# Reordering hand-written engine tables of a four-layer sequence kernel: the turned x, the first MLP product, and the gate and up products of one pass

## The reference

```
# layer 0
mx = layernorm(x) * (1 + sc_msa) + s_msa
i, f, g = bitlinear(mx, wi), sigmoid(bitlinear(mx, wf)), bitlinear(mx, wg)
o = hgrn_scan(silu(i) * (1 - f), f)
o = rmsnorm(o) * silu(g)                      # u: the scan's output times the gate
x = x + g_msa * bitlinear(o, wo)
gate, up = split(bitlinear(mlp_in(x), wm1))
x = x + g_mlp * bitlinear(silu(gate) * up, wm2)
# layer 1
h = rmsnorm(x)                                # xn, turned to xT
z = h @ pre_w ;  g = smooth(z) * harmonic_gate
y = merge_w @ [h, style mixed by a cosine of g and style]
x = x + gelu(rmsnorm(y) @ ffn_w1) @ ffn_w2    # f1, gelu, f2
```

## Time and profile before

| | |
|---|---|
| median of 3 runs | 1957.49 us (1952.1 to 1957.84) |
| the profiled execution, device time | 1953.37 us |
| its span, first to last instruction | 1951.6 us |
| PE, DVE, ACT, POOL busy | 88%, 67%, 57%, 31% of the span |
| mean granted TensorE clock | 0.939 of full speed |

### The profile page before, as it was taken

How to read it: one execution, slowest core, us unless ns; L and a number is a source line. 1 busy time by engine, 2 the same in 40 slices (tenths; PEclk the granted TensorE clock), 3 DMA queues, 4 the chain that set the end, 5 groups by cost and what they waited for, 6 DMA issues and landing times.

```text
span 1951.6 us, 25700 instructions
## 1 busy us (share of the span) xinstructions
PE 1715.5 (88%) x8463; PEld 1015.6 (52%) x8463; DVE 1312.7 (67%) x2873; ACT 1112.6 (57%) x2118; POOL 611.0 (31%) x880
## 2 busy tenths in 40 slices
PE   2365576999989999988999999999999998999998
PEld 1144344667557657552445454544445444676766
DVE  5756877887876665577868686767686734656550
ACT  6644667878768763344675757565757564222221
POOL 0145655856645633610101010100001002334332
PEclk9755788989999999998999999999999999999999
DMA  9450000000000002303120303030303005000000
GB/s 375 123 167 1 24 6 20 20 1 20 15 1 14 20 4 67 66 18 68 26 47 11 61 2 71 2 68 5 68 5 68 5 3 152 3 11 22 12 22 22
DMA packets 94422, 83.57 MB, mean 43 GB/s; under 512 B 9881, under 2 KB 87842, under 8 KB 94034
## 3 DMA queue, kind: packets, MB, share of 16 engines
q1 hardware_dynamic: 94192, 81.91, 15.3%
q10 hardware_dynamic: 98, 0.03, 0.0%
HBM read 51.26 MB, written 5.09 MB: 29 GB/s over the span
## 4 chain that ended last, share of the span: by engine, by line
PE 41%; DVE 8%; ACT 6%; issue 1%; POOL 1%; POOLq 0%; DVEq 0%; ACTq 0%
PE k_psum L91 13%; PE k_psum L2536 6%; PE k_psum L2062 5%; PE k_psum L2123 5%; PE k_psum L2176 5%; PE k_psum L2053 4%; PE k_psum L97 3%; DVE l_small L2212 2%; ACT l_prob L2001 2%; ACT L2001 1%; ACT L2017 1%; ACT l_gu L2017 1%; DVE l_xn L2285 1%; DVE l_small L2199 1%; DVE l_xn L2287 1%
## 5 line engine op out<-in xcount | busy, mean ns | idle before, releaser
L2212 DVE TENSOR_REDUCE l_small<-k_psum 128x1 f32<-128x512 f32 x512 | 328.8, 684 | 124.6 <-PE k_psum L2176 121.7
L2001 ACT ACTIVATE l_prob<-k_psum 128x512 f32<-128x512 f32 x512 | 286.4, 596 | 196.6 <-PE k_psum L2053 193.4
L1985 POOL TENSOR_TENSOR k_x_res<-k_x_res,k_arena_a 128x256 f32<-128x256 f32 x32 | 23.3, 727 | 418.8 <-DVE k_arena_a L2256 418.8
L2062 PE MATMUL k_psum<-l_prob,l_v 128*32 128x512 f32 x1024 | 138.1, 612 | 0.2
L2123 PE MATMUL k_psum<-k_arena_a,l_gu 128*128 128x256 f32 x512 | 135.5, 393 | 0.7 <-ACT l_gu L2017 0.7
L91 PE MATMUL k_psum<-l_turned_over,k_arena_a 128*128 128x512 f32 x256 | 120.8, 596 | 4.2 <-ACT l_gu L2017 4.2
L91 PE MATMUL k_psum<-k_arena_b,l_w_f 128*128 128x512 f32 x256 | 123.9, 612 | 0.0
L1468 PE MATMUL k_psum<-l_w_f,k_arena_b 128*128 128x256 f32 x512 | 122.7, 386 | 0.2 <-ACT k_arena_b L1282 0.2
L91 PE MATMUL k_psum<-l_hT,k_arena_b 128*128 128x512 f32 x256 | 114.3, 592 | 0.0
L2536 PE MATMUL k_psum<-k_arena_b,l_gu 128*128 128x256 f32 x512 | 113.0, 379 | 0.0
L2123 PEld LDWEIGHTS k_psum<-k_arena_a,l_gu 128*128 128x128 f32 x512 | 97.9, 197 | 19.8 <-issue 2.2
(11 more groups left out here) (390 smaller groups left out, 3786.6 us busy)
## 6 DMA issues: line engine op xcount, KB each, us to landing
su_raw<-in_L_cond_wa SPq DMA_DIRECT2D x6, 1536.0 KB, 22.4
k_arena_b<-k_arena_c SPq DMA_DIRECT2D x32, 192.0 KB, 3.5
k_x_res<-in_x SPq DMA_DIRECT2D x1, 4096.0 KB, 19.7
k_arena_b<-k_arena_c SPq DMA_DIRECT2D x32, 128.0 KB, 3.2
out<-k_x_res SPq DMA_DIRECT2D x8, 512.0 KB, 2.9
l_mod_mlp<-mod SPq DMA_DIRECT2D x8, 384.0 KB, 3.6
l_qT<-k_arena_c SPq DMA_DIRECT2D x16, 192.0 KB, 3.7
l_kT<-k_arena_c SPq DMA_DIRECT2D x16, 192.0 KB, 3.2
```

Source lines behind the costliest of these rows:

```text
L2001: act.activation(prob[:, s % 2, j, :], psum[:, 2 + n % 2, :], ACT.Exp, scale=float(HD) ** -0.5).then_inc(exp_ready.sem, 1)
L2062: last = pe.matmul(psum[j * BLOCK:(j + 1) * BLOCK, 4, :], v[e % 2][:, kt, at:at + BLOCK], prob[:, n % 2, j, :], start=(kt == 0), stop=(kt ...
L2212: dve.tensor_reduce(mx[:, n % T, n // T:n // T + 1], psum[:, s_bank(e, n), :], AX.X, ALU.max).then_inc(max_ready.sem, 1)
```

## The change

Only the order of entries in three tables changes; no instruction is added or taken away, and every entry keeps its waits.

On ScalarE `xT` 0 moves from before `proj` 2 to behind it. On PE `turn` 0 moves behind `proj` 2 and one `f2` entry, and `turn` 1 behind `xq` 3 and one `f2` entry. In the middle of PE's pass `f1` 0 moves ahead of `up` 4, and `up` 5, 6 and 7 move behind `merge` 1, `f1` 1 and `merge` 2. On VectorE `h` 2 moves ahead of `s`, `rinv` and `base` 0; `u` 0, `h` 3, `u` 1, `merge` 0, `h` 4, `u` 2 are dealt anew, and `amax` 3 moves behind `u` 2.

```
 ACT_TURN
-    ... ("ssq2", 0, 0), ("ssq", 2, 2), ("xT", 0, -1),
-    ("proj", 2, 1), ("xl2", 3, 0), ("xT", 1, -1), ...
+    ... ("ssq2", 0, 0), ("ssq", 2, 2),
+    ("proj", 2, 1), ("xT", 0, -1), ("xl2", 3, 0), ("xT", 1, -1), ...
 PE_TURN
     ... ("gate", 5, 0),
-    ("mods", 1, 1), ("up", 4, 0), ("f1", 0, -2), ("up", 5, 0), ("gate", 6, 0), ("merge", 1, -1), ("gate", 7, 0), ("up", 6, 0), ("f1", 1, -2),
-    ("up", 7, 0), ("merge", 2, -1), ("f1", 2, -2), ...
+    ("mods", 1, 1), ("f1", 0, -2), ("up", 4, 0), ("gate", 6, 0), ("merge", 1, -1), ("up", 5, 0), ("gate", 7, 0), ("f1", 1, -2), ("up", 6, 0),
+    ("merge", 2, -1), ("up", 7, 0), ("f1", 2, -2), ...
-    ("f2", 2, -2), ("xq", 2, 2), ("f2", 3, -2), ("turn", 0, 0), ("proj", 2, 2), ("f2", 4, -2), ("turn", 1, 0), ("xq", 3, 2), ("f2", 5, -2),
+    ("f2", 2, -2), ("xq", 2, 2), ("f2", 3, -2), ("proj", 2, 2), ("f2", 4, -2), ("turn", 0, 0), ("xq", 3, 2), ("f2", 5, -2), ("turn", 1, 0),
     ("proj", 3, 2), ("pre", 0, 0))
 DVE_TURN
-    ... ("h", 1, -2), ("xw", 3, 0), ("s", 0, -3), ("rinv", 0, -3),
-    ("base", 0, -3), ("h", 2, -2), ("u", 0, -1), ("amax", 3, 0), ("u", 1, -1), ("h", 3, -2), ("merge", 0, -3), ("u", 2, -1), ("h", 4, -2),
+    ... ("h", 1, -2), ("xw", 3, 0), ("h", 2, -2), ("s", 0, -3), ("rinv", 0, -3),
+    ("u", 0, -1), ("base", 0, -3), ("h", 3, -2), ("u", 1, -1), ("merge", 0, -3), ("h", 4, -2), ("u", 2, -1), ("amax", 3, 0),
     ("amaxh", 0, -2), ("u", 3, -1), ("h", 5, -2), ...
```

## The result

The changed kernel takes 1984.87 us (median of 4 runs, 1980.06 to 1988.55) against 1957.66 us before (4 runs beside them): 1.0142 times as long, 95% interval 1.0109 to 1.0175, 27.2 us by the medians. The forecast was 1972, slower, with a range from 1957 to 1990: the result lies inside it, 12.9 us above the forecast. The profiled execution took 1988.55 us, its span is 1986.8 us. It is the slowest of the four, and its trace is 35.2 us longer than that of the kernel before, 8 us more than the medians differ: what follows is read from this one pair of executions. The page's first part, as in the earlier trace rows, hides it: TensorE is busy 20 us longer in a span that is 35 us longer.

The account below looks back on a forecast made before the run. The bound was a pass as one ring through PE, VectorE, ScalarE and GpSimd. 3 x 4.4 + 1.0 + 2.2 + 2.2 - 0.6 - 1.5 = +16.5 us on 1953.4, plus 2, gave 1972; range 1957 to 1990.

Parts of the forecast that it names:

- The ring: Whole pass: dots, MLP middle, `hq`, ScalarE and GpSimd, next pass; lengthening any part lengthens every pass.
- The middle of a full pass: Passes 2, 3, 6: late `h` 4, `u` 2, `silu` 5 make `gate` 6 wait 2.5 us; 4.4 us lost per pass.
- Passes 4 and 5 and the held `s`: `s` held by GpSimd's `hw` 0; 2.71 us wait at `up` 3 goes, `o` 3 waits 1.5; -0.3 us each.
- The end: End of pass: `turn` 0's wait nearly goes, but `fi` 0 waits for `proj` 3; 0.25 us gained in 6 passes, -1.5.
- Passes 0, 1, 6 and 7: Passes 0, 1 and 7 lack parts: 1.0, 2.2 and 2.2 us longer; pass 6 like 2 and 3, 4.4 us.
- clock rival: Clock falls after the new wait at `gate` 6: 3.5 us in passes 2 to 6, 17 us more, 1989; chance 0.20.
- the held `s` could not decide: Rival, faster: passes 4 and 5 gain 4.45 us each if `gate` 6 starts no later than before; 1945, chance 0.08.
- the end did not pay the middle back: Rival, no difference: only PE's 1.93 us counts in passes 2, 3, 6, and the end gains 1.75; 1955, chance 0.10.

Follow-up runs that it names:

- experiment 3: Kernel before with only VectorE's new order (`h` 2 ahead of `s`, `rinv`, `base` 0; `u` 2 behind `h` 4): 1953.42 us, ratio 0.9988.
- (2): Kernel before with only TensorE's middle edit (`f1` 0 ahead of `up` 4; `up` 5, 6, 7 behind `merge` 1, `f1` 1, `merge` 2): 1972.45 us, ratio 1.0082.
- (10): Kernel before with TensorE's middle edit and, of VectorE's edit, only `u` 2 behind `h` 4: 1987.90 us, ratio 1.0166.
- experiment 9: Changed kernel without TensorE's middle edit, so the end edit and VectorE's new order together: 1953.22 us, ratio 0.9981 against the kernel before.
- (8): Changed kernel with `up` 5, 6 and 7 put back at their old places on TensorE: 1957.72 us, ratio 1.0012 against the kernel before.
- (7): Changed kernel with `up` 5 put back ahead of `gate` 6 on TensorE: 1963.02 us, ratio 1.0042 against the kernel before.
- experiment 1: Kernel before with only the edit at the end of the pass (`xT` 0, `turn` 0 and `turn` 1 moved): 1950.32 us, ratio 0.9971.
- experiments 5 to 8: Changed kernel with, in turn, `u` 2 back (1971.34 us), `silu` 5 ahead of `ssqu` 2 (1965.85), `up` 5 back (1963.02), `up` 5 to 7 back (1957.72).
- experiment 4: Kernel before with only `h` 2 ahead of `s`, `rinv`, `base` 0 and `u` 0 ahead of `base` 0 on VectorE: 1959.01 us, ratio 1.0012.

## Why the prediction was right, point by point

**The ring.** Right. `hq` starts 6.43 us after `h` 7 in pass 3 of both kernels, and the ends of passes 3 and 4, where all engines have their full load, changed by 0.04 and 0.01 us: nothing behind `qsh` took up the lateness. From `h` 0 to `h` 0 pass 3 took 77.4 us, 77 forecast.

**The middle of a full pass.** Right in each step. Counted from `gate` 5, `gate` 6 was forecast at 425.95 - 420.83 = 5.12 and came at 5.12; `u` 2 at 3.44 and 3.45, `silu` 5 at 4.30 and 4.31. Pass 2 grew by 4.41 for 4.4. Pass 3 by 4.72, by two things that nearly cancel: `gate` 5 came 1.17 us sooner after `h` 0 (13.91 for 15.08), and `h` 7 came 1.42 later after `gate` 5 than forecast, since `merge` 1 and what follows ran partly at the lower clock (2.79 us for 1.89). The forecast wait of 2.5 us was 2.38. In passes 2, 4 and 5, where the clock stays up behind `gate` 5, `h` 7 comes 13.62 us after `gate` 5, and 434.36 - 420.83 = 13.53 was forecast.

**One cause or two.** The prediction followed one chain without asking which edits it needs; the runs show that the whole of it needs both ends, and half of it TensorE's edit alone. VectorE's order with `u` 2 behind `h` 4 costs nothing alone (experiment 3), TensorE's edit 0.82% alone (2), that edit and `u` 2 behind `h` 4 1.66% (10). Going the other way from experiment 9, over ratios from three sets of runs and so to some 0.2% each, `f1` 0 ahead of `up` 4 adds 0.31% (8), `up` 6 and 7 behind the products 0.30% (7), and `up` 5 behind `merge` 1 a whole 1.00% (the changed kernel), since it leaves TensorE nothing to do in the wait for `silu` 5 and then owes VectorE its `up`.

**Passes 4 and 5 and the held `s`.** Right in pass 4: +0.38 for -0.3, the 2.71 us and the half-clock `f1` went, `o` 3 waited 1.74 us (forecast 1.5) and `gate` 6 2.38. Pass 5 came out alike (+0.46) by luck: there the first instruction of `s` took 0.80 us and `o` 3 did not wait, but with 3.4 us at the lower clock ahead of it `gate` 5 came 13.49 us after `h` 0, as in pass 4 (13.45). In the kernel before, `gate` 6 of pass 4 started at 499.37, later than the 498.9 of the prediction. The held instruction is `s` now, here VectorE's and GpSimd's timelines in pass 4 of the changed kernel.

```profile
505.45 1.93 DVE L1727 TENSOR_TENSOR l_small<-l_small 128x4 f32<-128x4 f32 x1
507.42 0.65 DVE L1728 TENSOR_SCALAR l_small<-l_small 128x4 f32<-128x4 f32 x1
```

```profile
505.00 2.36 POOL L1040 TENSOR_TENSOR k_arena_a<-k_arena_a,l_n_m 128x1024 f32<-128x1024 f32 x1 [0.95 <-ACT l_junk_h L1151]
```

`s` ends at 507.38, 0.02 us after `hw` 0. By the rule of the Trainium skill's page "SBUF — State Buffer", section "SBUF: two separate sides", which lets the two engines lock each other out for a whole instruction, it would; the trace agrees with 1.93 us for four elements a row.

**The end.** The sum was right (-1.75 for -1.5) by luck, the step was not. In pass 3 the waits came as forecast: at `turn` 0 0.47 us are left, and `fi` 0 waits 1.23 for `proj` 3 (TensorE's timeline in the changed kernel).

```profile
481.48 0.66 PE L97 MATMUL k_psum<-k_ident,l_xn 128*128 128x128 f32 x4 [0.47 <-ACT l_xn L1248]
...
489.36 0.41 PE L97 MATMUL k_psum<-k_ident,k_arena_c 128*128 128x128 f32 x2 [1.23 <-ACT k_arena_c L1183]
```

That `fi` 0 waits for `proj` 3 behind `ssq2` 3, which waits for GpSimd, holds in passes 3 and 4, but it gave 0.04 us and nothing there, not 0.25 in each of six passes. What it missed is that `ssq2` 1 to 3 also stand behind `xT` 1. Where TensorE is late, they wait for `turn` 1 and not for GpSimd: in the kernel before at the end of pass 2, where ScalarE's timeline has

```profile
395.11 0.60 ACT L1255 ACTIVATE k_arena_b<-k_psum 128x512 f32<-128x512 f32 x1 [1.60 <-PE k_psum L97]
```

and the edit gains 1.81 us, and in the changed kernel in passes 5 and 6, where it loses 1.45 and 0.55. Alone the end gained 5.7 us by the medians; its one trace shows part of that as a shift of the lower clock (experiment 1).

**Passes 0, 1, 6 and 7, and the clock.** Here the terms were too small: +19.8 us for 9.8. Passes 0 and 7 missed 1.4 of it, passes 1 and 6 8.6. The prediction named no wait at `gate` 6 in passes 0 and 1, which have no `f1`; it was 2.38 and 2.75 us, as in the full passes. And passes 1 and 6 have 7 us each more at the lower clock. At half speed that is 3.5 us of work lost in each, an estimate and an upper one: pass 2 of the changed kernel, with 6.8 us of it, took as long as pass 4 with none (27.13 and 27.07), since `gate` 5 came 13.5 us after `h` 0 in both.

Behind the wait at `gate` 6 the price can be read off. From `h` 4 to `h` 5 it is 5.1 us in passes 2, 4 and 5 of the changed kernel, where the clock stays up, and 6.4 to 6.5 in passes 3 and 6, where it falls for 3.4 us: 1.3 us. VectorE in pass 4, to be held against pass 3 above (435.00 and 441.45):

```profile
511.94 0.75 DVE L1608 SCALAR_TENSOR_TENSOR k_arena_a<-k_psum,l_small,k_arena_a 128x512 f32<-128x512 f32 x1 [0.94 <-PE k_psum L91]
...
517.08 0.75 DVE L1608 SCALAR_TENSOR_TENSOR k_arena_a<-k_psum,l_small,k_arena_a 128x512 f32<-128x512 f32 x1 [1.74 <-PE k_psum L91]
```

That is the prediction's clock rival, which gave it 3.5 us a pass in passes 2 to 6: it came in two of these five, with 1.3 us each. The other 3.4 us that pass 6 has more lie ahead of `gate` 5, so the new wait of that pass did not bring them; from `h` 0 to `gate` 5 the pass got 2.1 us longer. Sum: 16.5 forecast, 28.05 in the traces; of the 11.6 missed at most some 7 went to the clock in passes 1 and 6, by the estimate above, the rest in small shares over the other passes.

**The other rivals** fell: `gate` 6 was late in all passes from 0 to 6, so the held `s` could not decide, and the end did not pay the middle back.

**What stays open** is what sets the clock's place. The two kernels with the full wait at `gate` 6 have the most low time in the middles (53.5 and 51.2 us), and curing the wait in experiments 5 to 8 took 10 to 22 us of it away, which may be part of their gain; but the kernel before has 45.8 and experiment 4 49.4 with no such wait. Of one execution each, this doesn't settle how much of the 27 us the clock brought. No run changed the clock by itself.

## What to carry to other kernels

When entries of in-order tables are swapped, follow one late start through every queue that stands behind it: here five hand-overs over three engines could be forecast to a tenth of a microsecond, and an edit that costs nothing alone doubled the loss of another. Before a bank's emptying is put behind another wait, look whether the engine that wants the bank still has independent work in front of it; `up` 5 was that work, and its place alone decided 1.0%. Read the end of a stage in each pass, not in one: the same edit gained 1.8 us in one pass and lost 1.5 in another, because a different queue was last.

## What the runs showed of the hardware

A wait of TensorE was not always followed by the lower clock. In passes 2 to 6 of the changed kernel and of experiment 10 TensorE stood still for the same 2.38 us at `gate` 6, ten times; within the next 3 us the granted clock fell to the lower level five times and stayed at the higher one five times. Two windows behind that wait in the changed kernel, pass 3 and pass 4:

```profile
437.00:441.00 4.00, 3.66 (x12) 2.54 (x13) 1.39 (x2) 1.81 (x4) 0.00 (x0) 0.70 0.02 4
515.00:519.00 4.00, 4.00 (x16) 2.33 (x15) 2.27 (x5) 1.90 (x6) 0.00 (x0) 1.00 0.01 4
```

And it fell without any wait: in pass 6 of the kernel before, where TensorE goes from the 32 one-column products of `dots` straight on to the next `gate` and `up` products, busy throughout.

```profile
633.00:635.00 2.00, 2.00 (x11) 1.09 (x10) 1.87 (x6) 1.91 (x6) 1.11 (x2) 0.59 0.03 8
```

The Trainium skill's page "TensorE: Matmul & The Clock Gate", section "HAM oscillation — how this bites in real kernels", puts the lower clock down to idle gaps of TensorE, and to longer ones than these; the traces show it behind gaps of 2.38 us in five of these ten passes, and once without a gap. The place of such a stretch is worth as much as its length: 3.4 us of it in time that TensorE would have waited cost nothing (pass 4 of experiment 1), 3.4 us behind `gate` 6 cost 1.3, and on the whole of `f1` 0, 3.62 us long for 1.88, it cost 1.74.
